# A depthwise convolution moved from VectorE to diagonal 32x32 products on TensorE, in a fused two-layer kernel

## What is computed

```python
xz = xn @ in_proj_w.T + in_proj_b
xc, z = jnp.split(xz, 2, axis=-1)
kern = jnp.transpose(conv_w, (2, 1, 0))
xc = lax.conv_general_dilated(xc, kern, window_strides=(1,), padding=[(D_CONV - 1, 0)], ..., feature_group_count=D_INNER) + conv_b
u = _silu(xc)
x_db = u @ x_proj_w.T + x_proj_b
B_ssm, C_ssm = jnp.split(x_db, 2, axis=-1)
delta = jax.nn.softplus(u @ dt_proj_w.T + dt_proj_b)
y = _selective_scan(u, delta, -jnp.exp(A_log), B_ssm, C_ssm)   # h = exp(delta A) h + delta u B; y = h C, 16 states
y = (y + u * D_param) * _silu(z)
out = y @ out_proj_w.T + out_proj_b
```

## Time and profile before

| | us |
|---|---|
| median of 3 executions | 3182.5 (3182.36 to 3185.03) |
| profiled execution | 3180.75 |
| its span, first to last instruction | 3179.0 |
| ahead of the first scan | 146 |
| turns of the 16 batches | 151.3 for the one cut out below |

### The profile page before, as it was taken

The page is one execution under the profiler, slowest core; times in us unless marked ns, Lnnn a source line. Parts: engine busy times, 40 slices in busy tenths (PEclk is TensorE's granted clock), DMA queues, the critical chain, the costliest instruction groups (busy, mean ns, idle before and its releaser), DMA issues. The chain is left out here.

```text
span 3179.0 us, 47169 instructions
## 1 busy us (share of the span) xinstructions
PE 2799.8 (88%) x13205; PEld 1852.2 (58%) x13206; DVE 2488.6 (78%) x4112; ACT 2060.8 (65%) x3797; POOL 2156.5 (68%) x2202
## 2 busy tenths in 40 slices
PE   4777989898989898989889898989897789999998
PEld 2445555655555565656565555555655547777776
DVE  3599999999999999999999999999998632222222
ACT  3677777787867777777777777778675324444443
POOL 1378787787878687869687878788787514444443
PEclk8898999999999899999999999999898889999999
DMA  2043434343434343433434343434347323334433
GB/s 79 21 103 74 101 83 100 78 108 82 103 75 99 81 108 76 100 84 94 94 90 95 88 97 83 100 82 107 75 104 187 98 55 62 63 63 63 63 61 52
DMA packets 147356, 272.54 MB, mean 86 GB/s; under 512 B 19873, under 2 KB 78306, under 8 KB 147170
## 3 DMA queue, kind: packets, MB, share of 16 engines
q0 software_dynamic: 57840, 152.07, 26.8%
q1 hardware_dynamic: 79106, 109.65, 10.8%
q10 hardware_dynamic: 10224, 8.57, 0.8%
HBM read 107.16 MB, written 45.63 MB: 48 GB/s over the span
## 5 line engine op out<-in xcount | busy, mean ns | idle before, releaser
L914 POOL TENSOR_TENSOR dbu<-du,bbc 128x512 f32<-128x512 f32 x1024 | 1338.8, 1387 | 146.9 <-DVE h L1505 138.5
L1505 DVE TENSOR_TENSOR_SCAN h<-bank,dbu 128x512 f32<-128x512 f32 x1024 | 1220.4, 1210 | 48.1 <-ACT bank L1134 45.5
L1134 ACT ACTIVATE bank<-region,amat 128x512 f32<-128x512 f32 x1024 | 702.5, 689 | 102.2 <-DVE h L1505 97.0
L697 PE MATMUL bank<-ident,h 128*128 128x128 f32 x4096 | 625.2, 288 | 118.7 <-DVE acc L1495 51.5
L697 PEld LDWEIGHTS bank<-ident,h 128*128 128x128 f32 x4096 | 494.4, 148 | 402.1 <-DVE acc L1495 134.8
L1118 ACT ACTIVATE hTc<-bank,cT 128x512 f32<-128x512 f32 x448 | 306.5, 684 | 235.2 <-PE bank L697 130.2
L1675 POOL DMA_INDIRECT out<-ye,ids x135 | 212.2, 1572 | 345.2 <-DMA out<-ye,ids 312.5
L1495 DVE SCALAR_TENSOR_TENSOR acc<-bank,cT,acc 128x512 f32<-128x512 f32 x576 | 416.4, 730 | 23.3 <-PE bank L697 21.8
L651 PE MATMUL bank<-x4T,w_su 128*128 128x512 f32 (+1 forms) x768 | 375.5, 610 | 9.9 <-ACT region L961 8.5
L900 POOL DMA_DIRECT2D acc<-hTc x224 | 203.1, 907 | 262.4 <-ACT hTc L1118 250.4
L1711 DVE SCALAR_TENSOR_TENSOR gg<-gt,bank 128x352 f32<-128x352 f32 x135 | 70.3, 520 | 383.6 <-ACT gt L1645 383.6
...
## 6 DMA issues: line engine op xcount, KB each, us to landing
...
bbc<-b_scratch SPq DMA_DIRECT2D x256, 256.0 KB
...
```

The source lines that it names most:

```text
L697: last = tr(scan[f"hT{s}.{t}"][:, m * P:(m + 1) * P], h[:, s % 2, m, t * P:(t + 1) * P], ident[:, :])
L914: g.tensor_tensor(dbu[:, n % 4, :], du[:, m, :], bbc[:, (b * NS + s) % NROW, :], ALU.mult).then_inc(S("dbu_ready"), 1)
L1134: f(db(n)[:, :], delta[:, 1 - par, m, :], ACT.Exp, scale=amat[:, m, s:s + 1]).then_inc(S("da_ready"), 1)
L1505: v.tensor_tensor_scan(h[:, s % 2, m, :], db(n)[:, :], dbu[:, n % 4, :], 0.0, ALU.mult, ALU.add)\
```

## The change

Three things are altered. The convolution: ScalarE adds the projection's bias in moving a block to SBUF (`xin_of`); TensorE multiplies it, for each tap k, by a diagonal matrix `cdiag`, as four 32x32 tiles at rows and output partitions j to j+32, over the time columns shifted by k, and sums the four taps in the bank that the projection had used (`conv_of`); ScalarE then takes the tanh from the bank to SBUF and adds the convolution's bias within the bank, and VectorE forms u with its operands exchanged. The conv taps and edges on VectorE and their constants are gone, and `cdiag` is built in their place. The table `AT` has new numbers for many steps. Some small tensors are placed on top of others (`eidi`, `rowi`, `runi`, `fencei` in `region`; `alog` on `amat`).

```diff
-        cwh, cbh = sb("cwh", [P, MC, TAPS]), sb("cbh", [P, MC])
-        cwsum, cbias = sb("cwsum", [P, MC, TAPS]), sb("cbias", [P, MC])
-        edge = sb("edge", [P, MC, TAPS - 1])
+        cdiag = sb("cdiag", [P, MC, TAPS, Q])
+        cbh = sb("cbh", [P, MC])
...
+                def conv_of(m):
+                    done(pe, "xin_ready", b, m)
+                    if b == 0 and m == 0:
+                        pe.wait_ge(cdiag_ready, 1)
+                    for k in range(TAPS):
+                        if k:
+                            yield k / 2
+                        for j in range(0, P, Q):
+                            last = mm(proj[f"in{m}", b][j:j + Q, k:T], cdiag[j:j + Q, m, k, :], ch[j:j + Q, m % 2, 0:T - k],
+                                      start=k == 0, stop=k == TAPS - 1)
+                    last.then_inc(S("conv_ready"), 1)
...
-                steps = [(AT["in_x"][m], in_proj(m)) for m in range(MC)] + [(AT["xBC_pe"], xBC_of()), (AT["dt_pe"][0], dt_proj(0))]
+                steps = [(AT["in_x"][m], in_proj(m)) for m in range(MC)] + [(AT["conv_pe"][m], conv_of(m)) for m in range(MC)]
+                steps = sorted(steps, key=lambda x: x[0]) + [(AT["xBC_pe"], xBC_of()), (AT["dt_pe"][0], dt_proj(0))]
...
-                def tap_of(m):
+                def xin_of(m):
...
-                    f(ch[:, m % 2, TAPS - 1:T], proj[f"in{m}", b][:, TAPS - 1:T], ACT.Identity, bias=cbias[:, m:m + 1],
-                      scale=cwh[:, m, TAPS - 1:TAPS])\
-                        .then_inc(S("conv_first"), 1)
+                    f(ch[:, m % 2, :], proj[f"in{m}", b][:, :], ACT.Identity, bias=in_b[:, m:m + 1]).then_inc(S("xin_ready"), 1)
...
-                    f(proj[f"in{m}", b][:, :], ch[:, m % 2, :], ACT.Tanh).then_inc(S("conv_tanh"), 1)
...
+                    f(ch[:, m % 2, :], proj[f"in{m}", b][:, :], ACT.Tanh, bias=cbh[:, m:m + 1])
+                    f(proj[f"in{m}", b][:, :], proj[f"in{m}", b][:, :], ACT.Identity, bias=cbh[:, m:m + 1]).then_inc(S("conv_tanh"), 1)
...
+                for m in range(MC):
+                    for k in range(TAPS):
+                        last = v.tensor_scalar(cdiag[:, m, k, :], id32, cw[:, m, TAPS - 1 - k:TAPS - k], None, ALU.mult)
+                last.then_inc(cdiag_ready, 1)
...
-                def conv(m):
-
-                    xz, lead = proj[f"in{m}", b], ch[:, m % 2, :]
-                    done(dve, "conv_first", b, m)
-                    v.scalar_tensor_tensor(lead[:, 0:TAPS - 1], xz[:, 0:TAPS - 1], cwh[:, m, TAPS - 1:TAPS], edge[:, m, :],
-                                           ALU.mult, ALU.add).then_inc(S("conv_tap"), 1)
-                    for k in range(1, TAPS):
-                        done(dve, "conv_tap", b, (TAPS - 1) * m + k - 1)
-                        v.scalar_tensor_tensor(lead[:, k:T], xz[:, 0:T - k], cwh[:, m, TAPS - 1 - k:TAPS - k], lead[:, k:T],
-                                               ALU.mult, ALU.add).then_inc(S("conv_tap" if k < TAPS - 1 else "conv_ready"), 1)
...
-                    v.scalar_tensor_tensor(u[:, m, :], proj[f"in{m}", b][:, :], 1.0, ch[:, m % 2, :], ALU.add, ALU.mult)\
+                    v.scalar_tensor_tensor(u[:, m, :], ch[:, m % 2, :], 1.0, proj[f"in{m}", b][:, :], ALU.add, ALU.mult)\
```

61 lines of the change are left out of this document (27 added, 34 removed).

## The result

| | before | after |
|---|---|---|
| median | 3182.4 us (3181.8 to 3185.0) | 3274.8 us (3273.5 to 3277.8) |
| span of the profiled execution | 3179.0 | 3271.6 |
| first scan | 146.1 | 161.3 |
| steady turn, mean of batches 1 to 13 | 151.0 | 156.8 |
| of it scans 0-7 / 8-27 / 28-31 / 32-63 | 15.8 / 48.7 / 7.7 / 78.8 | 16.1 / 51.7 / 7.6 / 81.4 |

The ratio is 1.029 (1.027 to 1.031): slower, where 3114 us was forecast, and above both the forecast's 3085 to 3150 and its outer bound of 3210. By the start times of VectorE's scans, of the 92.6 us (3271.6 - 3179.0) 15.2 are lost ahead of the first scan, 13 x 5.8 = 75 in the steady turns, and 3 in the other three turns together; what follows the last scan is 1.3 us shorter.

What follows compares the result with a forecast made beforehand. VectorE was taken as the bound, busy 144.3 of a 151.3 us turn. Thirteen steady turns at -4.8 us (-62), two lighter ones (-16) and the start (+10) gave -68: 3114 us against the median, range 3085 to 3150 (58%).

Steps and rivals of the forecast that it cites:

- rivals 1 and 2: Rival 1: the convolution's tiles on TensorE go one after another, 57 us in place of 16, 3630; 2 isn't described.
- The clock in scans 12 to 19: TensorE's granted clock there should rise above 0.65 to 0.72, as the added products fill the pauses.
- rival 3: The ring between ScalarE and TensorE takes all of the gain: +7.4 us a turn, 3210; chance 8%.
- -9.9: Four edges and twelve taps removed from VectorE in a steady turn, all on the path that sets the end.
- -2.7: VectorE's old wait for ScalarE's exponentials, nearly all in scans 16 to 19 of a turn, counted as gone.
- +1.5: Us a turn for TensorE getting the fourth block in scans 20 to 31 while VectorE loses 2.5; from 0 to 4.
- +0.8: Us a turn for one retimed step missing its place; the moved steps otherwise cost 0.
- Is 16 us hidden?: TensorE's 16 us of convolution a turn fit into pauses and VectorE's waits, with TensorE behind by some 4 us.
- the ring: Bias add waits behind x4, convolution for it, transposes behind that, then hTc, tanh and next exponential: 1.1 us a turn.
- What ScalarE gets: ScalarE's added steps, +2.8 us a turn, make VectorE wait 5.5 us in all, between 3.5 and 9.
- The start, +10: Ahead of the first scan TensorE is the bound, with some 2 us of pauses: +10 us, from 4 to 14.
- The light turns: Turns of batches 0 and 14, without the late or attention work that crowds ScalarE and TensorE: -8 us each.

Runs made afterwards that it cites:

- e6: The changed kernel with the convolution's input and diagonal weights in bf16, one instruction in place of two for each product: 3187.7 us, ratio 1.001.
- e1: The changed kernel with only one of the four taps on TensorE, the rest of the convolution left out: 3169.1 us, ratio 0.996.
- e5: The changed kernel with every step that the convolution does not touch at the due times of the kernel before: 3314.0 us, ratio 1.042.
- e13: e9 (fp32 taps, old late due times) with the four taps of a block one right after another: 3292.0 us, ratio 1.034.
- e8: The changed kernel with bf16 taps and the old due times for everything due after scan 28: 3161.9 us, ratio 0.994.
- e12: e8 without ScalarE's addition of the convolution's bias in the bank: 3134.8 us, ratio 0.984.
- e2: The changed kernel, fp32 taps, without ScalarE's addition of the convolution's bias in the bank: 3270.7 us, ratio 1.029.
- e9: The changed kernel, fp32 taps, with the old due times for everything due after scan 28: 3243.9 us, ratio 1.020.
- e3: The kernel before, convolution still on VectorE, with the new due times for every step that the convolution does not touch: 3310.4 us, ratio 1.040.

## Why the prediction was wrong

**What was right.** The taps: 0.44 us for four tiles, as priced from the earlier trace rows, so rivals 1 and 2 are out. The Trainium skill's TensorEngine Tiling (Array Packing), Restrictions and Gotchas, by which row tiles cannot access one bank at a time, did not hold for these four tiles. The clock in scans 12 to 19 (1.00 in the turn cut out), the bias add at 0.66 and the tanh at 0.69 us came as forecast. Both chains that the prediction named, TensorE's taps ahead of transposes and ScalarE's crowd ahead of exponentials, are there, but both cost more than even rival 3 gave them (3210).

**The terms against the turn.** The sum had -9.9 of VectorE's work, -2.7 + 5.5 = +2.8 of waits for ScalarE, +1.5 for TensorE and +0.8 for the retimed steps: -4.8 us. The table of waits has -7.5 of VectorE's busy time, +8.9 of waits ended by ScalarE (2.3 to 11.2), +4.7 of those ended by TensorE (2.2 to 6.9) and -0.3 of pauses under 0.15 us: +5.8. The 10.6 us between them are 6.1 behind ScalarE, 3.2 behind TensorE and 2.4 of work, less 1.1. (VectorE's instructions did lose 9.4 us in summed length. Their records overlap when they follow each other closely, and less so with waits between, which is the likely reason for 7.5; it was not tested.)

**The first step that failed: "Is 16 us hidden?", and its term of +1.5.** The taps are not hidden. By waits they cost 4.7, and by experiment more: e6, with 10.4 us less of them, has the turn 5.6 us shorter, and e1, with as much less, 7.3, a part of it on the way over ScalarE (waits 11.2 to 10.0). At 0.5 to 0.7 us for each microsecond the sixteen would cost 9 to 11 (an estimate from these two runs), where I had 1.5 and the 1.1 of the ring. The warning stood in the earlier trace rows: TensorE's work at full clock in scans 8 to 31 was 4.80 + 9.81 x 0.72 + 9.13 x 0.65 + 24.20 = 42.0 us. With 16 more it is 58.0, and the stretch lasted 56.8, so VectorE's gain had no room. I cut the stretch in two instead, scans 4 to 15 and 20 to 31, and in each let TensorE be "behind by some 4 us", as if the first backlog were paid back before the second. That the stretch then took 58.5 us is in part luck: e5 and e13, with the same 16 us of taps, took 64 and 62 us for these scans (means of the steady turns, 59 in the changed kernel), so the sum is only a lower bound.

**The second: "What ScalarE gets", and its term of +5.5.** VectorE was to wait some 6 us a turn for exponentials; it waits 10.8, and still 9.5 with three of four taps gone (e1). So most of this wait isn't passed on from the taps. In scans 12 to 15 ScalarE is busy for 11.4 us a turn in the changed kernel and in e1 alike (8.9 before), and in e1 that is 11.4 of 12.5; I had counted 10.6 from the exponential of scan 13 to that of scan 16. Of its added work, the step in the bank is worth 1.6 us a turn with cheap taps (e8 to e12), and 0.8 with fp32 taps (e2). What makes up the rest, ScalarE's old work, the order of its steps or the bf16 taps that are left, no run parts.

**The term of +0.8 for the retimed steps.** I took the moved steps to be in work that waits for nothing, from busy times; which they are not. With the new convolution the late due times cost 2.1 us a turn (e9) and the early ones are worth 4.8 (e5 to e9), together a gain of 2.7; with the old convolution the new table costs 8.9 (e3). So the table's worth depends on where the convolution is, and the terms can't simply be added.

**The start, +10.** It took 15.2. In the two stretches of the earlier trace rows TensorE no longer pauses (below); the price of fp32 over bf16 taps is 8.8 of it (161.3 to 152.5 in e6). The other 6 appear with bf16 taps on either table (152.5 and 152.3) and with the new table alone (152.2); what delays them wasn't looked for.

```profile
76.00:86.00 10.00, 10.00 (x51) 3.47 (x49) 0.14 (x1) 4.32 (x8) 0.00 (x0) 0.93 0.01 2
86.00:96.00 10.00, 10.00 (x71) 2.58 (x70) 1.83 (x3) 3.74 (x8) 0.00 (x0) 1.00 0.01 2
```

**The light turns.** Batches 0 and 14 were to gain 8 us each. Batch 0 lost 3.1 and batch 14 gained 2.5; why wasn't looked for.

In all, of the 161 us between forecast and result 13 x (5.8 + 4.8) = 138 are in the steady turns, 5 in the start and 17 in the two light turns.
